# A decoder layer with 48 experts: records scattered into expert slots and loaded as plain rows, and the gate-up product on unsplit 32-bit operands

## The chip, the cores and the metric

One core of a Trainium2 chip runs the whole layer as one program. The metric is device microseconds of that program, the median of several runs. One more execution was profiled; its span runs from the first to the last instruction.

## The reference

A layer over x of shape 32 x 128 x 512 (32 batches of 128 tokens), in three steps, all in 32-bit floats:

```python
x = x + attention(layernorm(x))              # differential attention, 4 heads, rotary positions
x = x + cross(layernorm(x), ctx_2048, mask)  # 128 context rows of each batch
x = x + experts(layernorm(x))

# experts, T = 4096 tokens
logits = x @ gate.T                 # experts that are not kept get -inf: 48 are left
top_v, top_i = top_k(softmax(logits), 8); top_v /= sum(top_v)
pos = running count of earlier picks of the same expert      # in token order
valid = pos < 192                   # CAP: an expert takes its first 192 tokens
gu = xb[e, pos] @ gate_up[e].T      # 512 -> 2 x 192
h = silu(g) * u
final[tok] += top_v * (h @ down[e].T) if valid               # 192 -> 512
```

4096 tokens make 32768 picks, 683 for each expert on average, and 192 of each are kept. On these inputs every expert fills: 9216 records are valid. They lie in the first 14 batches: 1024 in each of batches 0 to 3, 979 to 828 in batches 4 to 7, 648, 453 and 257 in batches 8 to 10, 97 in the next three and none after batch 13 (counted from the reference's routing on its inputs).

## The kernel before

There are two stages. Every engine has its own queue in a fixed order, written out by hand; semaphores couple them.

**Main stage.** Loop turn j works on six batches at once, one in each step: norm (batch j), project (j-1), attend (j-2), cross (j-3), route (j-4), slots (j-5). In the step `route` the normed row of 128 tokens is written to `row` (line 831), in `slots` the 48 weights are added behind it (line 774). SyncE stores `row` to the tensor `xw` in HBM (line 415). GpSimd scatters the token's number into `table`, one 4-byte element for each of 8 picks (eight indirect DMAs of 128 indices in each turn, line 492); a pick with no slot has an index out of bounds and is skipped. GpSimd also computes the inverse roots (`rstd`, lines 502 and 519) between the scatters.

**Expert stage.** Loop turn j works on four experts: gather (e = j), turn (j-1), up (j-2), down (j-3). For one expert:

- gather: GpSimd fetches 192 rows of `xw` in two indirect DMAs (line 534) with indices from `slot_table`, into `rows` (in the buffer `w_raw`), two experts deep.
- turn: TensorE transposes the rows (line 1256, eight 96x96 blocks, called T here), ScalarE and VectorE split them into `rows_high` and `rows_low`. ScalarE and VectorE split the gate-up weights too (lines 672 and 1021).
- up: TensorE forms the gate-up product (line 1243, called G) of split operands: three products of fp32r pieces, 3 x 4 contraction blocks x 3 output blocks = 36 matmuls of 192 columns.
- down: TensorE forms the down product (line 1274, called W), two halves of five matmuls with 512 columns; two of the ten contract over 64 partitions only. ScalarE and VectorE scale the result into `y` (lines 698 and 1056), and GpSimd adds it to the output in HBM by two indirect DMAs with accumulation (line 552). Those of the next expert wait until these have landed (line 546).

In one turn TensorE's queue has G of expert j-2, then T of j-1, then W of j-3. SyncE loads `gu_sb` (768 KB for one expert, line 424) once the split of the expert two back is made, and the down weights (512 KB, lines 430 and 433). The names `second` and `rowsT1` are the semaphore steps "G is done" and "T is done".

Of the kernel before, what the change touches and what calls it, by code (L numbers as in the profile page):

```python
# [8 lines left out]
FP32 = mybir.dt.float32  # L9
# [8 lines left out]
P = 128  # L18
# [19 lines left out]
ROW = DM + E  # L38
SLOTS = HS * 2 * E
# [36 lines left out]
def decoder_layer(nc, x, ctx_rows, ctx_t, mask, weights, lambdas, subln, gate, gate_up, down_proj,  # L76
# [6 lines left out]
    xw = nc.dram_tensor("normed_rows_and_weights", (T + CAP, ROW), FP32, kind="Internal").ap()  # L83
    table = nc.dram_tensor("token_of_slot", (SLOTS, 1), I32, kind="Internal").ap()

    stack = ExitStack()
    with stack:
# [37 lines left out]
        spare_ids = sb("spare_ids", [HS, E, 2], I32)  # L125
# [4 lines left out]
        zeros = qk_both[0:HS, 0:2 * ROW]  # L130
# [66 lines left out]
        second_half = sb("second_half", [P, E])  # L197
        address = sb("address", [P, E])
        address2 = sb("address2", [P, E])
# [4 lines left out]
        token_id = sb("token_id", [P, 2], I32)  # L204
# [3 lines left out]
        dn_sb = sb("dn_sb", [P, 2, DM])  # L208
        dn2_sb = sb("dn2_sb", [P, 2, DM])
        assert 2 * (INTER - P) == P  # L210
        slot_table = sb("slot_table", [HS, E * 2], I32)
        gather_idx = sb("gather_idx", [HS, 2, 2], I32)
# [5 lines left out]

        def split_buffers(w):
            flat = w[:, :, :, :].rearrange("p m c n -> p (m c n)")  # L220
            at = 0
            for parts, *shape in ((P, 2, KC, 2 * INTER), (P, 2, KC, CAP), (P, 2, 1, DM), (P, 2, 1, DM),
                                  (P, 2, 1, CAP), (P, 2, 1, CAP)):
# [3 lines left out]
        gu_high, rows_high, dn_high, dn2_high, h1_high, h2_both = split_buffers(w_high)  # L227
        gu_low, rows_low, dn_low, dn2_low, h1_low, _ = split_buffers(w_low)
# [34 lines left out]
        setup_a = Steps(sem("setup_by_scalar"), "exp")  # L263
        s_spare = sem("spare_rows_written")
# [3 lines left out]
        d_row = [sem("records_stored0"), sem("records_stored1")]  # L268
# [28 lines left out]
        slt_v = Steps(sem("slots_vector"), "wsum winv fits weights half addr addr2 key slot8 none slots token")  # L297
        d_gu = [sem("gate_up_loaded0"), sem("gate_up_loaded1")]
        d_dn = [sem("down_loaded0"), sem("down_loaded1")]
        s_table = sem("slot_table_loaded")  # L300
        d_rows = [sem("rows_gathered0"), sem("rows_gathered1")]
# [4 lines left out]
        wgu_a = Steps(sem("gate_up_weights_scalar"), "high")  # L306
        wgu_v = Steps(sem("gate_up_weights_vector"), "low")
# [3 lines left out]
        ffn_a = Steps(sem("rows_scalar"), "high0 high1")  # L311
# [1017 lines left out]
```

## Time and profile before

| what | us |
|---|---|
| median of 3 runs (lowest to highest) | 1315.12 (1312.09 to 1326.86) |
| span of the profiled execution | 1216.7 |
| time outside that span (median less span) | 98.4 |
| first transposes of the expert stage start at | 735.7 |
| busy in the span: TensorE, VectorE, ScalarE, GpSimd | 1068.3, 888.6, 599.7, 661.2 |

Of the profiled execution only its span is recorded, no time of its own. So its time is taken as the span plus the 98.4 us that separate span and median; that part holds no instruction. A change in the span is carried over to the median one to one.

### The profile page before, as it was taken

The page shows a single profiled execution, that of the slowest core. Times are in us where ns is not written, and L with a number is a line of the kernel's source. Part 1 is how long each engine was busy: PE and PEld are TensorE (multiplying, and loading weights), DVE is VectorE, ACT ScalarE, POOL GpSimd, SP SyncE. Part 2 cuts the span into 40 slices and gives each one's busy share as a digit, 9 for nine tenths or more (in the row PEclk, how much of TensorE's full clock was granted, in tenths as well). Part 3 has the DMA queues.
Part 4 walks back from the last instruction along what each step waited for, and adds up shares of the span by engine and source line. Part 5 has one row for each costly group of instructions (what it writes and reads, how often), then busy time and mean ns, then how long its engine had stood idle before and what let it go on. Part 6 is the DMA issues. An engine that isn't in the chain of part 4 may idle for free.

```text
span 1216.7 us, 25344 instructions
## 1 busy us (share of the span) xinstructions
PE 1068.3 (88%) x6474; PEld 836.4 (69%) x6474; DVE 888.6 (73%) x2526; ACT 599.7 (49%) x1703; POOL 661.2 (54%) x627
## 2 busy tenths in 40 slices
PE   5989999999999999999999617898998898799985
PEld 4777777777777777777777406666776676577763
DVE  5788888888888888889888525666666666557662
ACT  3545555555554545454545204554555555446552
POOL 2115656565656566566665564554555655545553
PEclk9999999999999999999999757999899989989897
DMA  7112221313131313131212045988888989878884
GB/s 258 35 63 88 65 95 53 105 53 105 53 105 53 105 53 105 53 102 56 96 54 89 19 116 166 241 194 230 209 222 225 238 217 232 226 179 231 213 202 61
DMA packets 76505, 160.07 MB, mean 132 GB/s; under 512 B 18672, under 2 KB 18672, under 8 KB 75968
## 3 DMA queue, kind: packets, MB, share of 16 engines
q1 hardware_dynamic: 51136, 119.24, 31.4%
q0 software_dynamic: 25344, 40.54, 16.2%
q8 instruction: 11, 0.18, 0.1%
q14 instruction: 14, 0.11, 0.0%
HBM read 122.30 MB, written 37.43 MB: 131 GB/s over the span
## 4 chain that ended last, share of the span: by engine, by line
PE 27%; issue 25%; POOL 21%; DMA 14%; DVE 10%; POOLq 1%; ACT 1%; DVEq 0%; SPq 0%
DMA w_raw<-normed_rows_and_weights,gather_idx 12%; POOL token_of_slot L492 11%; PE ps L1274 11%; PE ps L1243 10%; POOL rstd L502 6%; DVE qk_both L918 5%; PE ps L1256 3%; DVE diff L913 2%; POOL qk_rot L515 2%; PE ps L1104 1%; POOL rstd_h L519 1%; DMA gu_sb<-in_weights 1%; POOL w_raw L534 1%; PE ps L1089 0%; DVE qk_both L1056 0%
## 5 line engine op out<-in xcount | busy, mean ns | idle before, releaser
L492 POOL DMA_INDIRECT token_of_slot<-token_id,slot_idx x256 | 254.8, 995 | 76.1 <-issue 66.5
L552 POOL DMA_INDIRECT layer_out<-qk_both,scatter_idx x96 | 155.4, 1619 | 176.7 <-DMA layer_out<-qk_both,scatter_idx 118.7
L502 POOL TENSOR_TENSOR rstd<-mv,neg_half 128x1 f32<-128x1 f32 x96 | 80.1, 834 | 166.3 <-DVE mv L859 84.3
L534 POOL DMA_INDIRECT w_raw<-normed_rows_and_weights,gather_idx x96 | 107.5, 1120 | 45.4 <-issue 32.3
L1104 PE MATMUL ps<-w_high,xn_high 128*128 128x512 f32 x384 | 114.0, 419 | 0.7 <-ACT xn_high L567 0.7
L1256 PE MATMUL ps<-ident,w_raw 96*128 96x96 f32 x384 | 42.9, 257 | 80.9 <-DMA w_raw<-normed_rows_and_weights,gather_idx 80.8
L602 ACT ACTIVATE probs<-ps,neg_max_s 128x128 f32<-128x128 f32 x256 | 89.9, 377 | 43.4 <-DVE neg_max_s L815 43.4
L1104 PE MATMUL ps<-w_low,xn_high 128*128 128x512 f32 x384 | 107.9, 403 | 0.0
L1104 PE MATMUL ps<-w_high,xn_low 128*128 128x512 f32 x384 | 107.2, 401 | 0.0
L1243 PE MATMUL ps<-w_high 128*128 128x192 f32 x576 | 98.3, 296 | 2.6 <-DVE w_low L1008 2.6
L1008 DVE TENSOR_TENSOR w_low<-ps,w_high 128x384 fp32r<-128x384 f32 x96 | 49.3, 552 | 65.9 <-ACT w_high L567 62.7
L1256 PEld LDWEIGHTS ps<-ident,w_raw 96*128 96x128 f32 x384 | 35.1, 145 | 85.3 <-issue 57.7
L1243 PE MATMUL ps<-w_low,w_high 128*128 128x192 f32 x576 | 93.0, 286 | 0.0
L1274 PE MATMUL ps<-w_high 128*96 128x512 f32 x192 | 90.6, 472 | 2.0 <-DVE w_low L1008 2.0
L1243 PEld LDWEIGHTS ps<-w_high 128*128 128x128 f32 x576 | 82.1, 206 | 14.9 <-issue 14.9
L1243 PE MATMUL ps<-w_high,w_low 128*128 128x192 f32 x576 | 92.1, 284 | 0.0
L1274 PE MATMUL ps<-w_low,w_high 128*96 128x512 f32 x192 | 90.8, 473 | 0.0
L567 ACT ACTIVATE xn_t<-ps 128x512 f32<-128x512 f32 x64 | 38.3, 599 | 97.2 <-PE ps L1089 97.2
L1008 DVE TENSOR_TENSOR w_low<-gu_sb,w_high 128x1536 fp32r<-128x1536 f32 x48 | 83.7, 1745 | 0.8 <-ACT w_high L567 0.8
L567 ACT ACTIVATE w_high<-ps 128x384 fp32r<-128x384 f32 x96 | 42.3, 489 | 80.7 <-PE ps L1256 79.8
L1243 PEld LDWEIGHTS ps<-w_low,w_high 128*128 128x128 f32 x576 | 81.7, 205 | 0.0
L1104 PEld LDWEIGHTS ps<-w_low,xn_high 128*128 128x128 f32 x384 | 70.9, 191 | 14.4
(169 smaller groups left out, 2628.1 us busy)
## 6 DMA issues: line engine op xcount, KB each, us to landing
gu_sb<-in_gate_up SPq DMA_DIRECT2D x48, 768.0 KB, 6.4
dn_sb<-in_down_proj SPq DMA_DIRECT2D x48, 256.0 KB
dn_sb<-in_down_proj SPq DMA_DIRECT2D x96, 128.0 KB
normed_rows_and_weights<-row SPq DMA_DIRECT2D x32, 280.0 KB, 2.2
x_ln<-in_x SPq DMA_DIRECT2D x32, 256.0 KB, 3.1
x_res<-in_x SPq DMA_DIRECT2D x32, 256.0 KB, 3.3
ctx_t_sb<-in_ctx_t SPq DMA_DIRECT2D x32, 256.0 KB, 3.6
ctx_sb<-in_ctx_rows SPq DMA_DIRECT2D x32, 256.0 KB, 4.1
```

The costliest lines, as they stand in the source:

```text
L492: pool.indirect_dma_start(out=table, out_offset=bass.IndirectOffsetOnAxis(ap=slot_idx[:, s.parity, k:k + 1], axis=0), in_=token_id[:, s.pa ...
L502: pool.tensor_tensor(rstd[:, :], mv[:, 1:2], neg_half[:, 0:1], ALU.pow).then_inc(steps.sem, 1)
L534: pool.indirect_dma_start(out=rows[:, e.parity, h, :], out_offset=None, in_=xw, in_offset=bass.IndirectOffsetOnAxis(ap=gather_idx[:, e.par ...
L552: pool.indirect_dma_start(out=out, out_offset=bass.IndirectOffsetOnAxis(ap=scatter_idx[:, d.parity, h:h + 1], axis=0), in_=y[:, d.parity, ...
L567: act.activation(dst, src, ACT.Copy).then_inc(steps.sem, 1)
L602: last = act.activation(probs[:, s, h, :], blocks(banks_s[:, s, :])[:, h, :], ACT.Exp, bias=neg_max_s[:, s, h:h + 1], scale=INV_SCALING, a ...
L918: dve.tensor_tensor(buf[:, :, :, :].rearrange("p g r f -> p (g r) f"), qk, rope_tab[:, i:i + 1, :].to_broadcast([P, 4 * NH2, NF]), ALU.mul ...
L1008: return dve.tensor_tensor(dst, src, high.bitcast(FP32), ALU.subtract)
L1104: last = pe.matmul(dst, left[:, c, :], right[:, m, c, :], start=(n == 0 and c == 0), stop=(n == 2 and c == KC - 1))
L1243: last = pe.matmul(dst, left[:, u.parity, k, cols], right[:, u.parity, k, :], start=(n == 0 and k == 0), stop=(n == 2 and k == KC - 1))
L1256: last = pe.transpose(ps[:, h, c * HS:(c + 1) * HS], rows[:, t.parity, h, c * P:(c + 1) * P], ident[0:HS, 0:HS])
L1274: last = pe.matmul(dst, left[:, d.parity, 0, half], right[0:n, d.parity, 0, :], start=(i == 0), stop=(i == len(pairs) - 1))
```

## The change

`xw` and `table` go. The tensor `records` in HBM has a place of 561 words (512 normed values, 48 weights, the token's number) for each of 48 x 192 slots. It is first filled with blank records by one DMA from ScalarE's queue (20.7 MB). GpSimd's eight scatters of a turn now carry the whole record. In the expert stage the indirect gather is replaced by one plain load of 192 records, issued by SyncE. The gate-up weights and the rows are no longer split: G is a product of 32-bit floats, 12 calls in place of 36. The down weights come in one DMA, the second part in both partition halves, and all ten matmuls of W contract over 128 partitions. The gate-up buffer is free again when G has read it, so its load waits for that. The first expert weights are loaded within the main stage. One more turn of each loop is written out ahead of the loop.

```diff
-ROW = DM + E
-SLOTS = HS * 2 * E
+TOKEN = DM + E
+ROW = TOKEN + 1
+SLOTS = CAP * E
...
 SyncE
+            def load_gate_up(e):
+                if e.back(2).exists():
+                    sp.wait_ge(gup_t.sem, gup_t.after(e.back(2), "second"))
+                sp.dma_start(gu_sb[:, e.parity, :, :], gate_up[bass.ds(e.index * P, P), :, :])\
+                  .then_inc(d_gu[e.parity], 16)
...
+            def load_rows(e):
+                if e.back(2).exists():
+                    sp.wait_ge(ffn_t.sem, ffn_t.after(e.back(2), "rowsT1"))
+                    sp.wait_ge(ffn_w.sem, ffn_w.after(e.back(2), "weight"))
+                sp.dma_start(rows[:, e.parity, :, :].rearrange("p h n -> p (h n)"),
+                             records[bass.ds(e.index * CAP, CAP), :].rearrange("(p h) n -> p (h n)", h=2))\
+                  .then_inc(d_rows[e.parity], 16)
+            def load_experts():
+                sp.wait_ge(s_split_v, 3)
+                sp.wait_ge(s_spare, 16)
+                sp.wait_ge(s_empty, 16)
...
-                if s.exists():
-                    sp.wait_ge(slt_v.sem, slt_v.after(s, "weights"))
-                    sp.dma_start(xw[bass.ds(s.index * P, P), :], row[:, s.parity, :])\
-                      .then_inc(d_row[s.parity], 16)
+                if b["slots"].first():
+                    load_experts()
...
             for par in range(2):
                 sp.wait_ge(d_slot[par], 16 * 8 * NB // 2)
-            sp.dma_start(slot_table[:, :], table.rearrange("(p n) o -> p (n o)", p=HS)).then_inc(s_table, 16)
+            load_rows(Batch(0, 0, E))
+            load_rows(Batch(0, 1, E))
             load_gate_up(Batch(1, 0, E))
             with sp.Fori(1, E // 2 - 1) as pair:
                 for off in range(2):
                     load_gate_up(Batch(pair, off + 1, E))
+                    load_rows(Batch(pair, off, E))
                     load_down(Batch(pair, off, E))
...
 GpSimd
-                            in_=token_id[:, s.parity:s.parity + 1], in_offset=None,
+                            in_=row[:, s.parity, :], in_offset=None,
...
                 if s.first():
-                    pool.wait_ge(s_spare, 48)
+                    pool.wait_ge(s_empty, 16)
...
 ScalarE
+                    act.wait_ge(s_blank_rec, 1)
+                    act.dma_start(records.rearrange("(e p h) n -> p e (h n)", p=HS, h=2),
+                                  blank.unsqueeze(1).to_broadcast([HS, E, 2 * ROW])).then_inc(s_empty, 16)
...
-                    copy(gu_high[:, t.parity, :, :], gu_sb[:, t.parity, :, :], wgu_a)
...
 VectorE
                     if r.back(2).exists():
-                        dve.wait_ge(d_row[r.back(2).parity], moved(r.back(2), 1))
+                        dve.wait_ge(d_slot[r.back(2).parity], moved(r.back(2), 8))
                     dve.tensor_scalar(row[:, r.parity, 0:DM], x2[:, r.parity, :], mv3[:, 0:1], rstd3[:, :],
...
 TensorE
-                    pe.wait_ge(wgu_v.sem, wgu_v.after(u, "low"))
-                    pe.wait_ge(ffn_v.sem, ffn_v.after(u, "low1"))
+                    pe.wait_ge(d_gu[u.parity], moved(u, 1))
+                    pe.wait_ge(ffn_a.sem, ffn_a.after(u, "copied0"))
+                    pe.wait_ge(ffn_v.sem, ffn_v.after(u, "copied1"))
...
-                        pairs = [(gu_high, rows_high), (gu_high, rows_low), (gu_low, rows_high)]
+                        return product(dst, lambda k: gu_sb[:, u.parity, k, cols], lambda k: rows_t[:, u.parity, k, :])
...
                 if t.exists():
-                    pe.wait_ge(d_rows[t.parity], moved(t, 2))
+                    pe.wait_ge(d_rows[t.parity], moved(t, 1))
...
-                                 (h2_both, dn2_high, P), (h2_high, dn2_low, INTER - P)]
+                                 (h2_both, dn2_high, P), (h2_both, dn2_low, P)]
```

What stands on SyncE's queue in the loop of the expert stage, before: the load of gate-up weights and those of down weights, one expert after the other.

```order
87 L424 ISA [waits gate_up_weights_vector]
88 L424 DMA gu_sb<-in_gate_up 128x1536
89 L429 ISA
90 L430 ISA [waits down_weights_vector]
91 L430 DMA dn_sb<-in_down_proj 128x512
92 L433 ISA
93 L433 DMA dn_sb<-in_down_proj 64x512 x2
```

And there after the change (`w_raw<-slot_records` is the load of the rows, `gate_up_tensor` the semaphore of G):

```order
84 L388 ISA [waits gate_up_tensor]
85 L388 DMA gu_sb<-in_gate_up 128x1536
86 L399 ISA
87 L401 ISA [waits rows_vector_kept,rows_tensor]
88 L401 DMA w_raw<-slot_records 96x1122
89 L394 ISA [waits down_weights_vector]
90 L394 DMA dn_both<-in_down_proj 128x1024
```

The load of the rows has moved from GpSimd's queue to this one, where it stands behind a load that waits for G.

TensorE's queue in one turn of the expert loop, before (G from line 1243, T from 1256; W follows):

```order
469 L1243 MATMUL ps<-w_high 128x192 [waits gate_up_vector]
470 L1243 MATMUL ps<-w_high 128x192 x3
471 L1243 MATMUL ps<-w_low,w_high 128x192 x4
...
479 L1251 ISA
480 L1254 REGISTER_ALU [waits rows_gathered0]
481 L1256 MATMUL ps<-ident,w_raw 128x96 [waits rows_vector]
```

And after, one turn with the first matmuls of W (now line 1236):

```order
560 L1057 MATMUL ps<-w_raw,gu_sb 128x192 [waits gate_up_vector]
561 L1057 MATMUL ps<-w_raw,gu_sb 128x192 x11
562 L1210 ISA
563 L1218 MATMUL ps<-ident,w_raw 128x96 [waits rows_scalar,rows_loaded0]
564 L1218 MATMUL ps<-ident,w_raw 128x96 x3
565 L1218 MATMUL ps<-ident,w_raw 128x96 [waits rows_vector]
566 L1218 MATMUL ps<-ident,w_raw 128x96 x3
567 L1222 ISA
568 L1223 REGISTER_ALU [waits down_weights_vector]
569 L1236 MATMUL ps<-w_high 96x512 [waits down_scalar,gate_up_vector]
```

G has 12 calls in place of 36; the order G, T, W is the same, and T still waits for its rows.

## Rows read from the trace of the kernel before

**Rows 1.** The page: TensorE's granted clock in 40 slices, in tenths.

```profile
PEclk9999999999999999999999757999899989989897
```

**Rows 2.** The chain of waits, from the last scatter on: start us, us, what.

```profile
723.69 2.09 DMA token_of_slot<-token_id,slot_idx
...
735.70 1.55 PE ps L1256 x8
...
738.51 7.28 PE ps L1243 x36
...
778.13 0.66 PE ps L1256 x8
778.79 2.84 PE ps L1274 x10
782.41 6.47 DMA w_raw<-normed_rows_and_weights,gather_idx
788.99 1.35 PE ps L1256 x8
790.34 3.87 PE ps L1274 x10
794.21 4.20 PE ps L1243 x36
...
854.39 7.32 PE ps L1243 x36
```

**Rows 3.** Indirect DMAs on GpSimd: duration ns min/median/max, first and last start us.

```profile
L492 POOL DMA_INDIRECT token_of_slot<-token_id,slot_idx x256: 966/974/1243, 97.7 to 723.7; - x128
L534 POOL DMA_INDIRECT w_raw<-normed_rows_and_weights,gather_idx x96: 962/1015/2353, 728.9 to 1179.6; - x96
L552 POOL DMA_INDIRECT layer_out<-qk_both,scatter_idx x96: 1413/1452/3418, 757.3 to 1208.3; - x96
```

**Rows 4.** Stretches of 2 us: busy, granted clock, DMA share, GB/s.

```profile
786.00:788.00 2.00, 0.00 (x0) 0.00 (x0) 0.76 (x3) 0.17 (x1) 0.00 (x0) 1.00 0.80 225
790.00:792.00 2.00, 2.00 (x8) 1.00 (x6) 1.62 (x4) 1.22 (x4) 1.70 (x2) 0.50 1.02 237
732.00:734.00 2.00, 0.00 (x0) 0.00 (x0) 0.00 (x0) 0.00 (x0) 1.64 (x2) 0.50 1.02 381
```

**Rows 5.** TensorE in time: matmuls of unsplit 32-bit floats, then transposes.

```profile
408.85 1.15 PE L1094 MATMUL ps<-ctx_t_sb,xn_t 128*128 128x128 f32 x8
409.84 0.60 PE L1089 MATMUL ps<-ident,diff 128*128 128x128 f32 x4
...
415.12 1.10 PE L1222 MATMUL ps<-ctx_sb,xprobs_t 128*128 128x512 f32 x2
416.16 0.63 PE L1089 MATMUL ps<-ident,xn 128*128 128x128 f32 x4
```

**Rows 6.** DMA issues: count, KB each, us from issue to landing.

```profile
gu_sb<-in_gate_up SPq DMA_DIRECT2D x48, 768.0 KB, 6.4
...
ctx_t_sb<-in_ctx_t SPq DMA_DIRECT2D x32, 256.0 KB, 3.6
ctx_sb<-in_ctx_rows SPq DMA_DIRECT2D x32, 256.0 KB, 4.1
```

**Rows 7.** SyncE in time, main stage: two loads issued one behind the other.

```profile
420.81 0.33 SPq L405 DMA_DIRECT2D ctx_t_sb<-in_ctx_t  x1
421.24 0.38 SPq L407 DMA_DIRECT2D ctx_sb<-in_ctx_rows  x1
```

**Rows 8.** VectorE and SyncE in time, expert stage: a load that waited for VectorE.

```profile
1007.55 1.75 DVE L1008 TENSOR_TENSOR w_low<-gu_sb,w_high 128x1536 fp32r<-128x1536 f32 x1
...
1009.86 0.34 SPq L424 DMA_DIRECT2D gu_sb<-in_gate_up  x1
```

**Rows 9.** GpSimd and VectorE in time, main stage: the last scatter of a turn, the next row.

```profile
419.80 0.97 POOL L492 DMA_INDIRECT token_of_slot<-token_id,slot_idx  x1 [0.31 <-issue]
...
422.23 0.55 DVE L831 TENSOR_SCALAR row<-x,mv,rstd 128x512 f32<-128x512 f32 x1 [0.47 <-POOL rstd L502]
```

More of the change, by code:

```diff
@@ L524, in _ @@
             turns(pool, turn)
-            def gather(e):
-                if e.exists():
-                    pool.wait_ge(ffn_i.sem, ffn_i.after(e, "index"))
-                if e.back(2).exists():
-                    pool.wait_ge(ffn_t.sem, ffn_t.after(e.back(2), "rowsT1"))
-                    pool.wait_ge(ffn_w.sem, ffn_w.after(e.back(2), "weight"))
-                settled(pool)
-                for h in range(2):
-                    pool.indirect_dma_start(
-                        out=rows[:, e.parity, h, :], out_offset=None, in_=xw,
-                        in_offset=bass.IndirectOffsetOnAxis(ap=gather_idx[:, e.parity, h:h + 1], axis=0),
-                        bounds_check=T + CAP - 1, oob_is_err=True).then_inc(d_rows[e.parity], 16)
             def expert_turn(b):
-                g, d = b["gather"], b["down"]
-                if g.exists():
-                    gather(g)
+                d = b["down"]
                 if d.exists():
@@ L667, in expert_turn @@
                 t, u, d = b["turn"], b["up"], b["down"]
-                if t.exists():
-                    act.wait_ge(d_gu[t.parity], moved(t, 1))
-                    if t.back(2).exists():
-                        act.wait_ge(gup_t.sem, gup_t.after(t.back(2), "second"))
-                    copy(gu_high[:, t.parity, :, :], gu_sb[:, t.parity, :, :], wgu_a)
                 if u.exists():
@@ L680, in expert_turn @@
                 if t.exists():
-                    for h in range(2):
-                        act.wait_ge(ffn_t.sem, ffn_t.after(t, f"rowsT{h}"))
-                        if t.back(2).exists():
-                            act.wait_ge(gup_t.sem, gup_t.after(t.back(2), "second"))
-                        copy(rows_high[:, t.parity, :, h * HS:(h + 1) * HS],
-                             ps[:, h, 0:KC * HS].rearrange("p (c n) -> p c n", c=KC), ffn_a)
+                    act.wait_ge(ffn_t.sem, ffn_t.after(t, "rowsT0"))
+                    if t.back(2).exists():
+                        act.wait_ge(gup_t.sem, gup_t.after(t.back(2), "second"))
+                    copy(rows_t[:, t.parity, :, 0:HS], ps[:, 0, 0:KC * HS].rearrange("p (c n) -> p c n", c=KC), ffn_a)
                 if u.exists():
@@ L1239, in gate_up_block @@
                         cols = slice(m * P, (m + 1) * P)
-                        pairs = [(gu_high, rows_high), (gu_high, rows_low), (gu_low, rows_high)]
-                        for n, (left, right) in enumerate(pairs):
-                            for k in range(KC):
-                                last = pe.matmul(dst, left[:, u.parity, k, cols], right[:, u.parity, k, :],
-                                                 start=(n == 0 and k == 0), stop=(n == 2 and k == KC - 1))
-                        return last
+                        return product(dst, lambda k: gu_sb[:, u.parity, k, cols], lambda k: rows_t[:, u.parity, k, :])
                     for m in range(2):
```

161 lines of the change are left out of this document (64 added, 97 removed).

## The prediction, made before the changed kernel ran

> **What bounds the kernel now.** I read the page first for the two stages, then the chain of waits, then single stretches in time. The clock of TensorE is full through the main stage, dips between the stages and stays near nine tenths in the expert stage [rows 1]. The main stage ends with GpSimd's last scatter, started at 723.69 and landed 2.09 us later; the first transposes of the expert stage start at 735.70 [rows 2]. From there to the end at 1216.7 it is 481 us.
>
> The expert stage has a steady period, and I take it from the scatter-adds, two for each expert [rows 3]: 96 of them, the first at 757.3, the last at 1208.3. The two of one expert start about 1.75 us apart (1.45 of the median plus 0.3 between), so 47 periods take 1208.3 - 1.75 - 757.3 = 449.3 us, **9.56 us per expert**. TensorE's own work in a turn is 4.20 (G, 36 matmuls) + 0.66 (T) + 2.84 (W) = 7.70 us at full clock [rows 2]. The rest is waiting: the chain has gathers of some 6.5 us in it [rows 2], most of which lies under G, since a gather is issued by GpSimd independently of G. The reader should see that T of one expert stands directly behind G of the one before on TensorE's queue, so whether the rows are there when G ends decides the turn.
>
> **The loads of the expert stage.** This is the part that decides. After the change SyncE's queue has, for expert e: the gate-up load of expert e+1, then the rows of e. The gate-up load of e+1 waits for `second` of e-1, that is for the end of G(e-1). TensorE's queue has G(e-1) and directly behind it T(e), which waits for the rows of e. So the load of the rows can't be issued before G(e-1) ends, and TensorE has nothing else until they have landed. Their own conditions (T and the weights of e-2) were met a turn earlier; only the place in the queue holds them back. I call this wait D. Its terms:
>
> - SyncE reacts: VectorE's split ended at 1007.55 + 1.75 = 1009.30, SyncE's load for which it waited started at 1009.86, so 0.56 us [rows 8].
> - The gate-up load, 786 KB in thousands of bytes, lies ahead of the rows. Two loads of 262 KB issued 0.43 us apart [rows 7] land after 3.6 and 4.1 us [rows 6], the second 0.93 us after the first: 0.28 MB/us, in order, and 3.6 - 0.93 = 2.7 us that don't scale. Gate-up: 2.7 + 2.8 = 5.5 us. The median measured for it is 6.4 us beside other traffic [rows 6], which will be thinner: I take 5.3.
> - The rows, 192 x 561 x 4 = 431 KB, follow it: 1.5 us at 0.28, 1.1 at the 0.381 MB/us that two gathers reached [rows 4]. I take 1.3.
>
> D = 0.56 + 5.3 + 1.3 = **7.2 us**. From below 0.56 + 2.1 (a scatter that moves nothing, [rows 2]) + 1.217 MB at 0.381 (3.2) = 5.9; from above 0.56 + 6.4 + 1.5 = 8.5. The Trainium skill says the same of the order (DMA: Bandwidth & Descriptors, "Queues, rings and completion order"): on each DMA engine the descriptors of one issuing queue are consumed in ring order. If instead the rows could pass the gate-up data, D would be some 4.5 us; the landings in [rows 6] agree with the page.
>
> **G on unsplit operands.** It has 12 calls. The rows of such matmuls count two instructions for a call (x8 for the four calls of a context score, x2 for one readout). Eight of 128 columns take 409.84 - 408.85 = 0.99 us, 0.124 each; two of 512 take 1.04, 0.52 each [rows 5]. A line between them gives 0.19 us at 192 columns, streaming alone 0.16; I take 0.183, so G = 24 x 0.183 = **4.4 us**, against 4.20 now: three times fewer calls buy nothing, since a split matmul of 192 columns costs only 0.117. Bounds 3.9 to 4.6.
>
> The Trainium skill (FP8 and Floating Point Precision, "TensorE Precision Notes") has true 32-bit as four passes through the array. Against three products of one pass that would be 4/3 of 4.20, 5.6 us, and the time would come out 44 x 1.2 = 53 us later than my forecast. The row's price per instruction contains what the passes cost here, and it decides.
>
> **T and W, and the clock.** T keeps eight transposes. W keeps ten matmuls, but the two over 64 partitions go: five per half at about 0.24 (as the other steps of 512 columns) make 2.5 us in place of 2.84, worth 0.3. What matters more is that TensorE now stands idle for 7 us in each turn. It stood still at 786 to 788 with the clock full; at 790 the granted clock was 0.50, the lower of the two levels, 1.2 GHz [rows 4]. T after that took 1.35 and W 3.87 us in place of 0.66 and 2.84, and G behind them was full again at 4.20 [rows 2]; but one G took 7.32, and the first one of the stage 7.28 [rows 2]. So after each D I price T at 1.35, W at 3.87 - 0.3 = 3.6, and one G in seven at 3 us more, 0.4.
>
> **Period.** G 4.4 + D 7.2 + T 1.35 + W 3.6 + 0.4 = **17.0 us**, against 9.56. The scatter-adds fit below it: issue 3.2 us and landing some 6 us, nine in all. That chain, which was level with the period before, is off the path. So are the splits of the gate-up weights on ScalarE and VectorE that go: 1.75 us per expert on VectorE [rows 8], worth nothing here. All 48 experts but 0, 1 and 47 have the wait: rows 0 and 1 are loaded ahead of the loop, and those of 47 behind no gate-up load. That leaves T(2) to T(46), 44 periods, 748 us.
>
> **Ends of the stage.** The last scatter lands at 725.8. The plain load follows at once, where before the table's load, an index and two gathers came in between: 431 KB land in about 4 us, T(0) at 729.6 (6 us earlier than now). T(0) at the low clock 1.55, a copy 0.6, G(0) at the low clock about 8, T(1) with its copy 1.5, G(1) about 5, then D: T(2) at about 753. T(46) at 753 + 748 = 1501. Behind it W(44), G(46), T(47), W(45), G(47), W(46), W(47) without such a wait, 23 us, one evacuation 1.7, the adds 2.3 and 8.4 (1208.3 to 1216.7): the span ends at **1536**, 319 us later than before.
>
> **The main stage.** The first price that no row shows is a scatter whose elements have 2244 bytes. GpSimd's time for a plain scatter of 128 four-byte elements is 0.974 us, for a gather of 96 rows of 2240 bytes 1.015, with the same least value (966 and 962 ns); the scatter-add of 96 rows takes 1.452 [rows 3]. The plain forms are nearest: I take 0.97, no change. At 1.45 it would be 0.48 x 8 = 3.8 us a turn, less some 0.9 of slack, 93 us over 32 turns. VectorE loses two small operations on the routing chain, 0.4 us a turn at best, 13 us in all, mostly under GpSimd's chain: I take 3.
>
> Second, the buffer `row`. VectorE's write of batch r must wait until the scatters of r-2 have landed. The last of them was issued at 419.80, and the write stands at 422.23, 2.43 us later [rows 9]; an empty scatter lands in 2.09 [rows 2], so late batches are covered by 0.3 us. With data each scatter moves 287 KB, four of them in 5 us; they should land 1 to 3 us later than that, on the first ten batches: 10 to 30 us, taken as 18. Third, the blank fill: 20.7 MB at 0.28 to 0.38 is 55 to 74 us of DMA from about 20 us on, and ScalarE has to issue thousands of descriptors; the first scatter, at 97.7 [rows 3], waits for it and so does SyncE. Bounds 0 and 25 us, taken as 5. Together the main stage is **20 us** longer (0 to 50, and 93 more in the case above).
>
> **Sum.** Span 1536 + 20 = 1556; with 98.4 around it 1654. Rounded for the unlike small terms: **1650 us**, 26% slower than the median of 1315.12.
>
> **Rivals.**
>
> 1. The clock doesn't come back within a turn. Then G costs 24 x 0.33 = 8 us, T 1.5, W 4.6, and with D 7.2 the period is 21.3: 44 x 4.3 = 190 us more, 1840. For it: 7 us idle in every turn, and G at 7.3 twice [rows 2]. Against it: after the other low stretches G was back at 4.20. Half of it (period 19) gives 1740.
> 2. D is short and the clock mostly full: D 5.9, T 0.66, W 2.5, G 4.4 give 13.5, 154 us less: 1500. For it: the DMA engines have less to do per us than now; against it the clock's fall after 3 us of idle.
> 3. Scatters of whole records cost GpSimd what the adds cost: 1650 + 93 = 1743.
> 4. **The other side, faster.** TensorE's own work is 4.4 + 0.66 + 2.5 = 7.6 us. If the rows were there when G ends, and the load landed sooner than the gathers, the period would fall to between 7.6 and the adds' chain of about 9: 47 periods save up to 92 us, the start 6, the main stage costs 20: 1240 to 1290. It decides at D below 2 us. The profile's gathers of over 6 us on the chain speak for the idea; the order of SyncE's queue speaks against it, for in it D can't be below one issue and one landing, 0.56 + 3.6. The Trainium skill (DMA: Bandwidth & Descriptors, "Issuing engine by pattern") calls the queue used for plain loads generally faster than GpSimd's; that shortens a load that is still issued too late.
> 5. The change moves the wait but D hides under something I overlooked, period unchanged at 9.5: 1330.
>
> **How the numbers follow.** Chances: forecast (period 15.5 to 18.5) 0.68; rival 1 in full or half 0.13; rival 2 0.09; rival 3 0.06; rival 4 0.03; rival 5 0.01. The likeliest one's own range is 1580 to 1720. To leave out no more than 2 in 10 I take in rival 2 and the half of rival 1 and of rival 3: 1490 to 1790. About 1% is what a measurement of this kernel can tell from no change. Faster by over 1%: 0.03; within 1%: 0.02, of which rival 5 is one half; slower 0.95.
>
> **What the profile of the changed kernel would show.** Period: the scatter-adds, first and last start, about 17 us apart per expert. D: TensorE's first transpose waiting for a DMA of the rows some 45 times, over 300 us in total, SyncE's load of gate-up weights waiting for TensorE, and in time the order end of G, two loads, transposes. G: 24 instructions in 4.4 us. Clock: fives and sixes in the second part of the page's row. GpSimd's scatters at 0.97 us. VectorE's line that writes `row` waiting for a DMA in the first ten turns only. The forecast is wrong if T finds its rows landed, or if the clock stays at one level throughout.

## The result, and the profile after

| | us |
|---|---|
| kernel before, median of 4 runs (lowest to highest) | 1317.76 (1312.09 to 1326.86) |
| changed kernel, median of 4 runs | 1729.24 (1723.17 to 1736.85) |
| ratio after : before, 95% interval | 1.3131 (1.3058 to 1.3204) |
| profiled execution after: time, span | 1723.17, 1721.4 |

Slower by 31%. The forecast was 1650, with 1490 to 1790 around it.

One thing about the numbers has to be said ahead of all others. The unchanged kernel takes about 1214 us in one group of runs and about 1320 to 1330 in the others, and stays at its level within a group. The profile that the prediction read (span 1216.7) is of the first sort; the times beside it, and all of the result, are of the second. Each of the three groups of the experiments ran on a chip of its own, so chip and session are not told apart here. Every profiled execution with a time of its own shows time = span + 1.8 us: nothing lies around the span, and the 98.4 us of the prediction are a difference between executions. Below, a kernel is compared only with the kernel before of its own group.

The page of the changed kernel: busy times, busy tenths of TensorE and GpSimd, granted clock [rows 1], use of the DMA engines.

```profile
PE 1132.6 (66%) x5898; PEld 904.7 (53%) x5898; DVE 774.5 (45%) x2366; ACT 515.2 (30%) x1607; POOL 542.1 (31%) x529
...
PE   6868888888888888886345445545445544544545
...
POOL 2135445555455554555311211211211111111212
PEclk9989989999999999996667767776766776776866
DMA  8964334312221121110244454453454454444444
```

The main stage fills the first half, at about the same clock as before (two eights among the nines). From slice 20 on TensorE is busy for half of the time and its granted clock is 0.6 to 0.8; GpSimd, busy for half of each slice before, has almost nothing to do.

The chain of waits between the stages (start us, us, what), to be laid beside [rows 2]:

```profile
835.58 2.08 DMA slot_records<-row,slot_idx
...
837.72 3.91 DMA w_raw<-slot_records
...
841.68 1.56 PE ps L1218 x8
...
843.97 7.13 PE ps L1057 x24
...
852.70 4.13 PE ps L1057 x24
...
857.73 6.22 DMA w_raw<-slot_records
...
864.00 1.54 PE ps L1218 x8
865.54 3.10 PE ps L1236 x10
```

The start came as worked out: 2.08 us to land, 3.91 for the plain load, T(0) at the low clock, G(0) 7.13, and T(2) 22.3 us after T(0) (23.4 forecast). Between the stages only the place is off: T(0) at 841.7 in place of 749.6.

One turn in the middle, by time; G of x24 is line 1057, T line 1218, W line 1236 [rows 5, 7, 8]:

```profile
1202.77 4.06 PE L1057 MATMUL ps<-w_raw,gu_sb 128*128 128x192 f32 x24
...
1204.58 1.61 POOL L539 DMA_INDIRECT layer_out<-qk_both,scatter_idx  x1 [14.30 <-DVE qk_both L1016]
...
1206.50 1.41 POOL L539 DMA_INDIRECT layer_out<-qk_both,scatter_idx  x1 [0.30 <-issue]
...
1207.02 0.33 SPq L388 DMA_DIRECT2D gu_sb<-in_gate_up  x1
...
1207.60 0.34 SPq L401 DMA_DIRECT2D w_raw<-slot_records  x1
1208.13 0.34 SPq L394 DMA_DIRECT2D dn_both<-in_down_proj  x1
1216.47 1.54 PE L1218 MATMUL ps<-ident,w_raw 96*128 96x96 f32 x8 [9.64 <-DMA w_raw<-slot_records]
```

This is the turn that the prediction described, in its order: G ends at 1206.83, the gate-up load starts 0.19 us later, the rows behind it, and T after 9.64 us of nothing. GpSimd's adds wait 14 us for VectorE's last evacuation: they are off the path.

The same stretch in windows of 2 us (busy of each engine with its count, granted clock, DMA share, GB/s) [rows 4]:

```profile
1208.00:1210.00 2.00, 0.00 (x0) 0.00 (x0) 0.00 (x0) 0.00 (x0) 0.00 (x0) 1.00 0.83 163
1210.00:1212.00 2.00, 0.00 (x0) 0.00 (x0) 0.00 (x0) 0.00 (x0) 0.00 (x0) 0.96 1.00 304
1212.00:1214.00 2.00, 0.00 (x0) 0.00 (x0) 0.00 (x0) 0.00 (x0) 0.00 (x0) 0.50 1.06 303
1214.00:1216.00 2.00, 0.00 (x0) 0.00 (x0) 0.00 (x0) 0.00 (x0) 0.00 (x0) 0.50 0.81 183
```

No engine works for 8 us, and the DMA engines are full in the middle of it, at 304 GB/s. The clock, full at first, is at its lower level (1.2 GHz) from about 1212 on, after TensorE had stood still since 1206.8.

Waits (us in total, times, longest), two indirect DMAs [rows 3], and DMA issues (count, KB each, us to landing) [rows 6]:

```profile
PE ps L1218 <- DMA w_raw<-slot_records: 436.9, 46, 21.4
```

```profile
L493 POOL DMA_INDIRECT slot_records<-row,slot_idx x256: 967/976/1472, 110.4 to 835.6; - x128
...
L539 POOL DMA_INDIRECT layer_out<-qk_both,scatter_idx x96: 1406/1408/1615, 870.5 to 1711.9; - x96
```

```profile
gu_sb<-in_gate_up SPq DMA_DIRECT2D x48, 768.0 KB, 7.1
dn_both<-in_down_proj SPq DMA_DIRECT2D x48, 512.0 KB, 9.1
...
w_raw<-slot_records SPq DMA_DIRECT2D x48, 420.8 KB, 8.4
```

T waits 46 times: 21.4 us before T(0), and 415.5 in the 45 turns T(2) to T(46), **9.23 each**. T(2) starts at 864.00 and T(46) at 1681.59, so the period is 817.6 / 44 = **18.58 us**; T(46) to the end is 39.8. (The adds, (1711.9 - 1.7 - 870.5) / 47, give 17.87, since their first and last turns are short. The experiments are compared by this second number, called "period by the adds".) A scatter of whole records costs GpSimd 0.976 us, as one of four bytes did. In the group of this profile a pause in most turns of the main stage, which the view of waits calls "remote", holds ScalarE (107.3 us in 26 turns) and VectorE.

### The profile page after: what moved, and what is told of

It reads as the page before. It is cut to its first block, busy times and chain, and to the rows that moved or that the text cites. A ratio compares the mean times of both kernels' runs of the same rounds, so it can differ in the third digit from the quotient of the medians.

```text
span 1721.4 us, 22946 instructions
## 1 busy us (share of the span) xinstructions
PE 1132.6 (66%) x5898; PEld 904.7 (53%) x5898; DVE 774.5 (45%) x2366; ACT 515.2 (30%) x1607; POOL 542.1 (31%) x529
## 4 chain that ended last, share of the span: by engine, by line
PE 28%; DMA 24%; issue 24%; POOL 15%; DVE 5%; SPq 1%; another core or an unknown queue 1%; POOLq 1%; ACT 1%; DVEq 0%
DMA w_raw<-slot_records 22%; PE ps L1057 12%; PE ps L1236 10%; POOL slot_records L493 8%; PE ps L1218 4%; POOL rstd L504 4%; DVE qk_both L894 2%; DVE diff L889 1%; POOL qk_rot L517 1%; SPq L388 1%; POOL rstd_h L521 1%; PE ps L1067 1%; DMA slot_records<-row,slot_idx 1%; DMA gu_sb<-in_weights 1%
## 5 line engine op out<-in xcount | busy, mean ns | idle before, releaser
L1218 PE MATMUL ps<-ident,w_raw 96*128 96x96 f32 x384 | 72.6, 368 | 436.9 <-DMA w_raw<-slot_records 436.9
L493 POOL DMA_INDIRECT slot_records<-row,slot_idx x256 | 255.8, 999 | 90.6 <-issue 81.3
L1004 DVE COPY w_raw<-ps 128x384 f32<-128x384 f32 x48 | 26.7, 557 | 475.2 <-PE ps L1218 475.2
L1057 PEld LDWEIGHTS ps<-w_raw,gu_sb 128*128 128x128 f32 x1152 | 198.4, 197 | 9.6 <-issue 2.5
L1057 PE MATMUL ps<-w_raw,gu_sb 128*128 128x192 f32 x1152 | 201.5, 333 | 1.7 <-DVE w_low L981 0.9
L1067 PE MATMUL ps<-w_high,heads_high 128*128 128x512 f32 x128 | 49.5, 521 | 75.1 <-ACT heads_high L553 72.2
L592 ACT ACTIVATE probs<-ps,neg_max_s 128x128 f32<-128x128 f32 x256 | 89.8, 376 | 14.2 <-DVE neg_max_s L791 12.6
L1067 PEld LDWEIGHTS ps<-w_high,xn_low 128*128 128x128 f32 x384 | 71.5, 193 | 14.8
L1067 PEld LDWEIGHTS ps<-w_high,heads_high 128*128 128x128 f32 x128 | 27.6, 237 | 92.0 <-ACT heads_high L553 84.4
L894 DVE TENSOR_TENSOR qk_both<-ps,rope_tab 128x1024 f32<-128x1024 f32 x64 | 75.1, 1215 | 0.9 <-PE ps L1067 0.9
L1067 PEld LDWEIGHTS ps<-w_high,xn_high 128*128 128x128 f32 x384 | 66.4, 192 | 10.4 <-ACT xn_high L553 1.1
```

What stands on the lines that cost most here:

```text
L493: pool.indirect_dma_start(out=records, out_offset=bass.IndirectOffsetOnAxis(ap=slot_idx[:, s.parity, k:k + 1], axis=0), in_=row[:, s.parit ...
L592: last = act.activation(probs[:, s, h, :], blocks(banks_s[:, s, :])[:, h, :], ACT.Exp, bias=neg_max_s[:, s, h:h + 1], scale=INV_SCALING, a ...
L894: dve.tensor_tensor(buf[:, :, :, :].rearrange("p g r f -> p (g r) f"), qk, rope_tab[:, i:i + 1, :].to_broadcast([P, 4 * NH2, NF]), ALU.mul ...
L1004: dve.tensor_copy(rows_t[:, t.parity, :, HS:CAP], ps[:, 1, 0:KC * HS].rearrange("p (c n) -> p c n", c=KC)).then_inc(ffn_v.sem, 1)
L1057: last = pe.matmul(dst, left(c), right(c), start=(c == 0), stop=(c == n - 1))
L1067: last = pe.matmul(dst, left[:, c, :], right[:, m, c, :], start=(n == 0 and c == 0), stop=(n == 2 and c == KC - 1))
```

## The experiments

Runs 1 to 4 were in the group with the kernel before at 1213.49 us (13 runs), 5 to 8 at 1320.14 (13), 9 to 12 at 1329.74 (21).

**1. The kernel before, again.** No edit.

> The kernel before, unchanged, profiled once more. Theory A (the main stage of the first profile was typical, and some 98 us lie outside the span): span near 1217 us, first transposes of the expert stage near 736 us, time some 98 us longer than the span. Theory B (the profiled execution had a shorter main stage than the timed ones): span within 5 us of the time, so near 1312, with some 95 us more in the main stage, and the same pause on all engines once in a turn that the changed kernel's trace shows at 509 to 511 us.

1214.39 us, span 1208.5; T(0) at 734.9; period by the adds 9.40. Theory B holds in its first half, span close to time; its longer main stage is absent, since this run stood in the other group. No line of its waits says "remote". The kernel before is the same program in all groups, so the 98.4 us are a difference between the group of the profile and that of the times.

**2. Rows first.** SyncE loads the rows of e+1, then the gate-up weights of e+1, a turn earlier than in the changed kernel.

```diff
+            load_rows(Batch(1, 0, E))
             load_gate_up(Batch(1, 0, E))
             with sp.Fori(1, E // 2 - 1) as pair:
                 for off in range(2):
+                    load_rows(Batch(pair, off + 1, E))
                     load_gate_up(Batch(pair, off + 1, E))
-                    load_rows(Batch(pair, off, E))
                     load_down(Batch(pair, off, E))
+            load_rows(Batch(E // 2 - 1, 1, E))
...
```

> The changed kernel with one move on SyncE's queue: the rows of expert e+1 are loaded ahead of the gate-up weights of e+1, one turn earlier, not behind them. Theory (the wait D is made by the place in the queue): T finds its rows landed, the period falls from 17.9 us to the larger of TensorE's 7.6 us and the chain of scatter-adds, about 8.3 (3.2 issue and 4.5 landing and 0.6): 8 to 9 us, so 44 x 9.4 = 410 us less, about 1315 in all. Rival (the DMA engines or the 32-bit loads are slow in themselves, whatever the order): the wait stays above 4 us in a turn and the time above 1500.

1280.08 us, ratio 1.054 (1.0485 to 1.0596); period 9.45, and T waits for its rows only at the stage's start. One load in another place of the queue carries almost all of the loss: against 17.84 in run 4, 8.4 us in each period. What is left, 5%, is in the main stage: T(0) at 804.1 against 734.9. There VectorE's write of `row` waits 84.7 us in 30 turns. Laid beside run 1, the distances between these writes are 15 us longer once, in the turn of the first scatter (GpSimd stands still for 12.6 us there, and starts it at 109.60; without the fill, in run 3, at 96.95), 29 us longer in the next eight turns together, whose scatters carry the most records, and 30 us in the others, where few or none are carried (74 in all, 69 of them left at T(0)). One of those late turns, by time:

```profile
605.64 0.34 SPq L419 DMA_DIRECT2D x_ln<-in_x  x1
606.30 0.33 SPq L424 DMA_DIRECT2D x_res<-in_x  x1
606.61 0.97 POOL L494 DMA_INDIRECT slot_records<-row,slot_idx  x1 [0.30 <-issue]
606.82 0.33 SPq L428 DMA_DIRECT2D ctx_t_sb<-in_ctx_t  x1
607.25 0.38 SPq L430 DMA_DIRECT2D ctx_sb<-in_ctx_rows  x1
610.29 0.55 DVE L808 TENSOR_SCALAR row<-x,mv,rstd 128x512 f32<-128x512 f32 x1 [1.95 <-DMA slot_records<-row,slot_idx]
```

The last scatter of the turn lies among four loads of SyncE, and the write stands 3.68 us after its start, not 2.43 as in [rows 9]. Between 440 and 690 us the turns are 21.5 to 22.4 us long, against 20.5 to 20.7 in run 1. That this wait is what lengthens them is argued from its size; no run in this group took it away.

**3. No blank fill.** The changed kernel without the DMA that writes blank records, and without the two waits for it; places that no token takes then keep what was there.

> The changed kernel without the blank fill of the records in HBM, and without the waits for it (left out: the 20.7 MB of blank records; every slot is filled by a scatter on these inputs). Theory (the fill costs a wait of GpSimd and SyncE at the first scatter, 13 us): 10 to 15 us less, about 1716. Rival (the fill also slows the loads and scatters of the first 120 us): 25 us less or more, 1704 or below. If the fill is hidden: no change.

1672.22 us; T(0) at 791.0, period 17.88. Beside run 2 (same main stage, with the fill) T(0) is 13 us earlier, as the theory had it, beside run 4 20 us. The times that the expectation named were those of the other group and can't be compared.

**4. The shorter lead.** The changed kernel with as many turns written out ahead of each loop as before.

```diff
-        PAIRS, FIRST, LAST = (NB + 6) // 2, 4, NB // 2
+        PAIRS, FIRST, LAST = (NB + 6) // 2, 3, NB // 2
-        EPAIRS, EFIRST, ELAST = (E + 4) // 2, 3, E // 2
+        EPAIRS, EFIRST, ELAST = (E + 4) // 2, 2, E // 2
```

> The changed kernel with as many turns written out ahead of the loops as before (3 and 2 in place of 4 and 3). Theory (the extra turns cost nothing): within 5 us of 1729. Rival (longer code brings the pauses in the main stage): pauses gone, up to 90 us less.

1694.87 us, ratio 1.3971 (1.3872 to 1.4071); T(0) at 811.0, period 17.84, the wait on `row` 89.8 us in 30 turns. The 1729 of the theory was a time of the other group. The rival fails as well: runs 2 and 3 have the long lead and no pauses either. The lead does nothing for the period. This is also the changed kernel's size where the pauses are absent: T(0) is 76 us later than in run 1.

**5. The changed kernel, again.** No edit.

> The changed kernel, unchanged, on the chip on which the kernel before takes 1213 us. Theory (the pauses of 2 to 4 us that every turn of the main stage shows in its first profile are not its own, but belong to that session, in which the kernel before took 100 us more as well): no pauses, first transposes of the expert stage near 811 us in place of 842, time near 1695. Rival (the pauses are the changed kernel's own): 842 and 1729 again.

1728.27 us, ratio 1.306 (1.2949 to 1.3172); T(0) at 843.4, the pauses there (104.7 us on ScalarE), period 17.94. The expectation was for the group of 1213 us, and this run came into another, so it doesn't decide between its two theories; runs 2 to 4, which have almost the same main stage and no pauses, speak against the rival. The main stage is longer in this group and the expert stage is not.

**6. Only G unsplit.** The kernel before, gathers and all, with G on unsplit weights and rows as in the changed kernel. As there, the gate-up load now waits for G and not for the split.

```diff
-                    copy(gu_high[:, t.parity, :, :], gu_sb[:, t.parity, :, :], wgu_a)
...
-                    left_by(gu_low[:, t.parity, :, :], gu_sb[:, t.parity, :, :],
-                            gu_high[:, t.parity, :, :]).then_inc(wgu_v.sem, 1)
...
-                        pairs = [(gu_high, rows_high), (gu_high, rows_low), (gu_low, rows_high)]
...
+                        return product(dst, lambda k: gu_sb[:, u.parity, k, cols], lambda k: rows_t[:, u.parity, k, :])
```

> The kernel before with one part of the change alone: G on unsplit 32-bit weights and rows, 12 calls, no splits of either; the gather, the small scatter and the down weights stay, and the gate-up load waits for G. Theory (G costs TensorE 4.0 to 4.2 us either way, and the period is the chain of scatter-adds with DMA engines that are nearly full): period 9.2 to 9.6 us, time within 1.5% of 1213. Rival (less work on ScalarE and VectorE shortens the turn): period 8.5 or less, 1170 or below.

1286.03 us, **ratio 0.9758 (0.9691 to 0.9825)**, period (1270.3 - 1.7 - 849.4) / 47 = 8.92: a gain, where none was expected. One G here, then the adds of run 6 and those of run 1 (ns min/median/max), and one add of run 1 beside VectorE:

```profile
1009.66 4.17 PE L1079 MATMUL ps<-w_raw,gu_sb 128*128 128x192 f32 x24
```

```profile
L553 POOL DMA_INDIRECT layer_out<-qk_both,scatter_idx x96: 1414/1453/1618, 849.4 to 1270.3; - x96
```

```profile
L552 POOL DMA_INDIRECT layer_out<-qk_both,scatter_idx x96: 1414/1453/3419, 756.3 to 1200.0; - x96
```

```profile
794.06 3.12 POOL L552 DMA_INDIRECT layer_out<-qk_both,scatter_idx  x1 [3.58 <-DMA layer_out<-qk_both,scatter_idx]
794.09 1.74 DVE L1008 TENSOR_TENSOR w_low<-gu_sb,w_high 128x1536 fp32r<-128x1536 f32 x1
```

G is no shorter (4.17 against 4.20). The gain is in GpSimd's chain of adds. Averaged over 40 turns in the middle, the two adds of an expert start 1.76 us apart here and 2.21 in run 1 (2.07 in the first profile); from the second to the first of the next expert, which waits for the landing, it is 7.29 here and 7.41 in run 1 (7.60). So most of the 0.6 us in run 1, and half of it in the first profile, lies in the adds themselves: 17 of the 96 adds in run 1, and 12 in the first profile, take 1.8 to 3.4 us on GpSimd. All of these 29 overlap VectorE's split of the gate-up weights, which is gone here, and with it every add over 1.62 us. Whether the rest comes from the landing, from the removed splits or from the later gate-up load was not taken apart.

**7. Rows late but ahead.** The load of the rows still waits for G, but stands ahead of the gate-up load.

```diff
                 for off in range(2):
-                    load_gate_up(Batch(pair, off + 1, E))
+                    sp.wait_ge(gup_t.sem, gup_t.after(Batch(pair, off + 1, E).back(2), "second"))
                     load_rows(Batch(pair, off, E))
+                    load_gate_up(Batch(pair, off + 1, E))
```

> The changed kernel with the two loads of a turn exchanged, but both still waiting for the end of G: the rows are issued as late as before, and the gate-up weights follow them. It tells the two parts of the wait D (9.6 us measured) apart. Theory (the rows' data come in order behind the gate-up data): D falls by what 786 KB take, 2.5 to 4 us, the period from 17.9 to 14 or 15, time near 1540. Rival (the landing is a latency that doesn't depend on what lies ahead): D and the time as they are, 1690.

1577.13 us, ratio 1.1952 (1.1833 to 1.2070); period 14.74. By time, and among its issues and waits:

```profile
1201.15 0.34 SPq L401 DMA_DIRECT2D w_raw<-slot_records  x1
1201.70 0.34 SPq L388 DMA_DIRECT2D gu_sb<-in_gate_up  x1
1202.22 0.33 SPq L394 DMA_DIRECT2D dn_both<-in_down_proj  x1
...
1207.47 1.54 PE L1219 MATMUL ps<-ident,w_raw 96*128 96x96 f32 x8 [6.49 <-DMA w_raw<-slot_records]
```

```profile
w_raw<-slot_records SPq DMA_DIRECT2D x48, 420.8 KB, 5.7
```

```profile
PE ps L1219 <- DMA w_raw<-slot_records: 288.9, 46, 21.3
```

(288.9 - 21.3) / 45 = 5.95 us a turn against 9.23 in the result and 9.27 in run 5 of the same group ((438.5 - 21.5) / 45). So D is 3.3 us of gate-up load ahead in the queue and 5.9 of a load that is issued too late. This agrees with the order that the Trainium skill gives (DMA: Bandwidth & Descriptors, "Queues, rings and completion order"): had the rows been able to pass the gate-up data, this edit would have changed nothing.

**8. Rows first, and a buffer of its own for the records.** As run 2; ScalarE copies `row` into `record`, and the scatters read that, so that VectorE's next write of `row` waits for the copy and not for DMAs.

```diff
-                            in_=row[:, s.parity, :], in_offset=None,
+                            in_=record[:, s.parity, :], in_offset=None,
...
+                    copy(record[:, o.parity, 0:TOKEN], row[:, o.parity, :], rec_a)
...
-                        dve.wait_ge(d_slot[r.back(2).parity], moved(r.back(2), 8))
+                        dve.wait_ge(rec_a.sem, rec_a.after(r.back(2), "copied"))
```

> The kernel with the rows loaded a turn earlier (1280 us), and the records scattered from a buffer of their own, filled by a copy on ScalarE, so that VectorE's next row doesn't wait for eight scatters. Theory (that wait, 84.7 us in 30 turns, is what lengthened a turn of the main stage from 20.6 to 21.8 us): period of the main stage back to 20.6, 40 to 50 us less, near 1235. Rival (the copy, or GpSimd's scatters, take its place): less than 15 us gained.

1321.74 us, ratio 1.0034 (1.0001 to 1.0068); period 9.34, T(0) at 849.9. The wait of the `row` write for the scatters is gone, but T(0) is no earlier than in run 5 (843.4) of the same group. The 1235 of the theory was a time of run 2's group. Since run 2 was in the other group, this says nothing yet of the buffer.

**9. Only G unsplit, again.** As run 6.

> The kernel before with only the gate-up product unsplit, a second time, to see whether its gain stands on another chip. Theory: of the 9.4 us of a period in the kernel before, only about 0.5 hung on the splits, and nothing else moved: period 8.9, time 0.97 to 0.98 of the kernel before on the same chip. Rival: the gain was a matter of that chip: ratio 0.99 to 1.01, period 9.3 to 9.5.

1301.0 us, ratio 0.9877 (0.9809 to 0.9945); period (1286.9 - 1.7 - 864.5) / 47 = 8.95. The gain stands, in a size of 1 to 2.5% over the two runs; the ratio lies just outside the theory's 0.97 to 0.98, the period, 8.95, is that of the theory and of run 6. It is the only version here that beats the kernel before.

**10. Rows first, again.** As run 2, beside the next.

> The changed kernel with the rows loaded a turn earlier, ahead of the gate-up weights, a second time, beside the version that adds the record buffer, on one chip. Theory: the wait of VectorE's row write for the last scatter (84.7 us in 30 turns) costs the main stage 40 to 60 us, so this kernel is 40 to 60 us slower than the one with the record buffer. Rival: what takes that wait away brings ScalarE a copy in each turn, and the two are within 15 us.

1329.35 us, ratio 1.0031 (0.9996 to 1.0067); T(0) at 858.8; period 9.42.

**11. Rows first with the record buffer, again.** As run 8.

> Rows first and records scattered from a buffer of their own, a second time, on the chip of the run ahead. Theory: T of the first expert 40 to 60 us earlier than there, the expert stage's period the same (9.3 to 9.5). Rival: T of the first expert at the same time within 15 us.

1323.79 us, ratio 1.0010 (0.9970 to 1.0051); T(0) at 848.5; period 9.37. Its T(0) is 10 us earlier than in run 10, not 40 to 60: the rival held, not my theory. Each T(0) is from one execution, that of run 10 its slowest; the medians differ by 5.6 us and the two intervals overlap, so no gain of the buffer is shown. In run 10 the wait on `row` between 200 and 800 us was only this, where run 2 had 70.6 us in 27 turns:

```profile
DVE row L808 <- DMA slot_records<-row,slot_idx: 7.6, 6, 2.0
```

The pauses of this group come ahead of that write and take the wait's place. What the buffer would bring where they are absent was not run. The expert stage of both is the chain of adds (run 11, chain of waits):

```profile
1162.36 1.41 POOL layer_out L543
...
1164.07 6.45 DMA layer_out<-qk_both,scatter_idx
...
1171.56 0.35 POOL layer_out L543
...
1173.27 8.14 DMA layer_out<-qk_both,scatter_idx
```

**12. Indexes late.** As run 11, with VectorE's write of the add's indexes moved from the head of its turn to just ahead of `y1`.

```diff
...
                 if d.exists():
+                    dve.wait_ge(ffn_w.sem, ffn_w.after(d, "tokens"))
+                    if d.back(2).exists():
+                        dve.wait_ge(d_add[d.back(2).parity], moved(d.back(2), 2))
+                    dve.tensor_scalar_add(scatter_idx[:, d.parity, :],
+                                          slot_table[:, bass.ds(2 * d.index, 2)], 0.0).then_inc(dwn_i.sem, 1)
                     dve.wait_ge(dwn_t.sem, dwn_t.after(d, "y1"))
```

> As the run ahead, but VectorE writes the add's indexes just ahead of its scaling of the second half of the outputs, behind h1, h2, the copy of the rows and the splits, so that none of these waits for adds to land. One theory: the period of the expert stage is the chain of adds themselves, each pair issued only when the pair before has landed (6.5 us from the second add's start, and 2.6 to 2.8 for the issue of the two and the waits between): the period stays at 9.3 and only VectorE's waits move, to that place. The other: the wait of h1 and h2 behind the indexes holds TensorE (5.1 us on VectorE in each turn): the period falls to 8.5 or less, and the time by 35 us or more.

1410.04 us, ratio 1.069 (1.0622 to 1.0759), period (1397.6 - 1.7 - 866.5) / 47 = 11.26. Both theories missed it. From its chain of waits:

```profile
1158.07 1.41 POOL layer_out L543
...
1159.78 8.58 DMA layer_out<-qk_both,scatter_idx
...
1168.49 0.06 DVE scatter_idx L1020
...
1168.60 0.76 DVE qk_both L1024
...
1171.11 9.24 DMA layer_out<-qk_both,scatter_idx
```

TensorE's wait for VectorE ahead of G fell from 78.7 us in run 11 to 1.7 in all, and the period rose all the same, so that wait did not set it. The chain is that of the adds, as the first theory had it, now with VectorE's index and `y1` in it; from a landing to the next add it is 1.04 us in both runs. What differs is the landing: along the chain, from 900 us on, it takes 7.9 to 9.7 us here (median 8.8) and mostly 6.2 to 7.4 in run 11 (median 6.6). In this version SyncE starts its three loads 0.2, 0.7 and 1.4 us after the second add (at 1007.90, loads at 1008.10, 1008.63, 1009.28), in run 8 2.0, 3.5 and 4.2 us after it. Loads that begin together with the adds would explain it; that was not tried by itself.

## Why the prediction was right, and where its terms were off

The step that decides held: the order of SyncE's queue puts the rows behind a load that waits for G, TensorE stands still in 45 turns, and the time rises by a quarter to a third. Run 2 shows the cause by removal (period 17.8 to 9.45), run 7 shows its two parts. None of the rivals came about. But the period, 18.58, is just beyond the 15.5 to 18.5 that the forecast's own case had, and 1729 is beyond that case's own 1580 to 1720: the time lies inside 1490 to 1790 only because the range was widened for rivals that did not happen.

| term | forecast | measured |
|---|---|---|
| D, wait of T for its rows | 7.2 (5.9 to 8.5) | 9.23 |
| T at the low clock | 1.35 | 1.54 |
| G, with the allowance for the clock | 4.4 + 0.4 | 4.14 (182.1 us busy in 44 turns) |
| W | 3.6 | 3.67 (rest of the period) |
| period | 17.0 | 18.58 |
| T(2) to T(46), 44 periods | 748 | 817.6 |
| T(0) | 749.6 | 841.7 |
| ends: T(0) to T(2), T(46) to the end | 23.4, 35 | 22.3, 39.8 |
| around the span | 98.4 | 1.8 |

**D** was the mis-sized term of the period, and outside its bounds. The reaction was overrated (0.19 in this turn for 0.56). The landing of the gate-up load was taken as 5.3 us because traffic would be thinner; it is 7.1. The traffic of that moment is not thinner: in those 8 us the windows sum to 1.9 MB, where I counted the gate-up weights and rows, 1.2. Next to them start the down weights (0.5 MB, SyncE, 1208.13) and the adds of two halves (0.4 MB of data, 1204.58 and 1206.50). The rate, 304 GB/s, is above the 280 of my estimate. So bytes are missing from the sum, by this reckoning; the loads were not separated by a run.

**T, W and the clock.** The low level after each D was right. G was back at the full clock as a rule (4.06 here, 4.14 on average), so the allowance of 0.4 went unused, and rival 1 with it. W starts at the lower level and regains the higher one in its course.

**G.** 24 instructions take 4.06 to 4.17 us, 4.4 forecast from the line through 128 and 512 columns. The Trainium skill counts four passes for true 32-bit (FP8 and Floating Point Precision, "TensorE Precision Notes"); the prediction's estimate from it, with one split matmul as the price of a pass, was 5.6 us, and the measurement decides against that as a price in time here. It does not say how many passes were made: an unsplit call takes 0.34 us in its two instructions, as long as 2.9 split matmuls of 0.117. "Three times fewer calls buy nothing" was true of TensorE. "The splits that go are worth nothing here" was true of the changed kernel, and false of the kernel before, as runs 6 and 9 show: 0.5 us a period by the adds.

**The scatters' price** on GpSimd (0.97) was right. **`row`**: "late batches are covered by 0.3 us" failed. Where no pauses are, the write waited in 30 turns, 84.2 to 89.8 us in total (runs 2 to 4), and not 18 us in the first ten. In the result itself it waited 18.9 us in 10 turns, seven of them before 350 us, much as forecast; that is luck, since the pauses cover the others. I had counted what the scatters move, and not the four loads of SyncE among which the last one lies in every turn; that these loads delay its landing is likely, and not shown. **The fill** cost 13 to 20 us, not 5. Together the changed main stage was 69 to 76 us longer in the first group (14 forecast: 20, less 6 at the join). In the others it is 13 us longer, as much as the fill costs beside run 2, each taken within its group: T(0) at 843.4 (run 5) against 830.6 (run 6), and 858.8 (run 10) against 845.5 (run 9); runs 6 and 9 have the main stage of before. There the pauses stand in the place of the wait on `row`. So of the 411 us between the medians, T(0) to the end has nearly all: 879.7 against the 481 of [rows 2], 399; the 13 us of the main stage are the rest.

**98.4 around the span** was wrong as a thing and of use as a number. The span that I started from and the median are of different groups. The term stood in for the pauses, and the 92 us that T(0) came too early in the forecast nearly cancel it; what is left, 69 us of the 1723.2 that were profiled over the 1654 of the sum, is nearly all the period. A range worked out with either alone would have been off by 100 us.

## What to carry to other kernels

Before a load is put on another queue, write down what stands ahead of it there and what that waits for: a load whose own conditions were long met cost 8.4 us in each of 45 turns, because it stood behind a load that waits for the end of G, and TensorE had nothing else to do after G. Count for such a wait all bytes that start in the same few microseconds, those of other queues and those issued behind it too (here the sum without them was 2 us short; that they are the reason was not tested). And where a change bundles several edits, time the small one alone: here G without splits was a gain of 1 to 2.5% inside a loss of 31%.

## What of the hardware was not expected

- An indirect scatter of 128 records of 2244 bytes takes GpSimd no longer than one of four bytes (medians 0.976 and 0.974 us), and a scatter-add of 96 rows 1.41 to 1.45.
- A scatter-add that overlaps VectorE's split of the gate-up weights (two inputs, 128x1536, 1.74 us) can take GpSimd up to 3.4 us; without that split, in runs 6 and 9, none takes more than 1.62. In run 2, 40 of the 96 take more than 1.6 us (up to 2.9), all 40 beside the split of the down weights (128x512). An overlap alone does not do it: in run 12 most adds beside that split take 1.41.
- G as 24 unsplit instructions of 192 columns (4.06 to 4.17 us) and as 36 split ones (4.20) take the same time.
- One program differs by 9% between groups of runs. The difference stands in the trace as one pause of 2 to 4 us in most turns of the main stage (26 of 32 in the result) on ScalarE and VectorE, released by something "remote"; what it is stays open. In the changed kernel of the result one of them is

```profile
511.04 1.22 DVE L783 TENSOR_REDUCE neg_max<-ps 128x8 f32<-128x1024 f32 x1 [2.23 <-remote]
511.07 0.69 ACT L555 ACTIVATE heads_t<-ps,subln_sb 128x512 f32<-128x512 f32 x1 [4.15 <-remote]
```

It hides other waits of the same turn: between 200 and 800 us the wait on `row` was 70.6 us in one group and 7.6 in another, for the same kernel.
